# V as the second kind, second sums in four quarters, one power for two, and a reordered loop in a fused graph-transformer kernel

## The reference, cut to what matters

```python
h = logmap0(proj(xn))                       # per row
z = h @ w_qkv                               # 768 channels: q, k, v
t = relu(batchnorm(z))                      # statistics over all 6250 rows
s = grouped_pointwise(depthwise(t))         # groups of 32 channels
ai = rescale(concat(t, s))                  # one factor per row, from the row's sum of squares
q, k = relu(q), relu(k)
vk = einsum('ngdl,ngel->ngde', v, k)        # one position: v * (sum of k over its 32)
out = einsum('ngde,ngdl->ngdl', vk, q) / (sum(v, -1) + 1e-15)
fx = expmap(out_rescaled @ w_res + b_res)
x1 = x + graph + fx
x2 = x1 + experts(layernorm(x1))
```

## Time and profile before

| | us |
|---|---|
| median of 3 runs | 843.91 |
| lowest and highest | 840.88, 845.69 |
| the profiled execution | 845.02 |
| its span | 843.2 |
| TensorE busy | 789.9 |
| VectorE busy | 523.4 |
| ScalarE busy | 424.6 |
| GpSimd busy | 389.2 |

### The profile page before, as it was taken

How to read it: one execution, slowest core, us unless ns; L and a number is a source line. 1 busy time by engine, 2 the same in 40 slices (tenths; PEclk the granted TensorE clock), 3 DMA queues, 4 the chain that set the end, 5 groups by cost and what they waited for, 6 DMA issues and landing times. The chain is left out here.

```text
span 843.2 us, 15014 instructions
## 1 busy us (share of the span) xinstructions
PE 789.9 (94%) x5042; PEld 648.9 (77%) x5042; DVE 523.4 (62%) x1475; ACT 424.6 (50%) x959; POOL 389.2 (46%) x601
## 2 busy tenths in 40 slices
PE   5899999999799999999659889999999999999996
PEld 4678888888466667766436778888888888888885
DVE  7762488797578888788888643534444353535345
ACT  2466436889578888888647232323232323222230
POOL 2430778778068888887636601312222221312122
PEclk9899999999899999999969999999999999999999
DMA  9755122222011110211101040000000000000000
GB/s 213 192 152 152 40 58 56 55 52 52 8 48 43 55 57 25 64 42 51 45 7 33 19 125 13 17 21 22 16 25 13 24 13 25 13 25 14 25 20 30
DMA packets 35422, 41.32 MB, mean 49 GB/s; under 512 B 11520, under 2 KB 20696, under 8 KB 35339
## 3 DMA queue, kind: packets, MB, share of 16 engines
q1 hardware_dynamic: 22355, 30.71, 12.8%
q0 software_dynamic: 8000, 6.82, 3.8%
q10 hardware_dynamic: 4984, 2.79, 1.4%
HBM read 25.59 MB, written 14.60 MB: 48 GB/s over the span
## 5 line engine op out<-in xcount | busy, mean ns | idle before, releaser
L916 ACT ACTIVATE Z<-ps,b1s 128x250 f32<-128x250 f32 x200 | 93.5, 469 | 234.9 <-PE ps L1182 232.1
L1195 PE MATMUL ps<-Z 128*125 128x256 f32 x800 | 176.5, 379 | 0.0
L1182 PE MATMUL ps<-Z 128*128 128x250 f32 x800 | 173.6, 374 | 2.3 <-DMA Z<-in_w 2.3
L1195 PEld LDWEIGHTS ps<-Z 128*125 128x125 f32 x800 | 150.2, 188 | 22.2
L1182 PEld LDWEIGHTS ps<-Z 128*128 128x128 f32 x800 | 151.3, 189 | 20.5 <-DMA Z<-in_w 2.9
L978 PE MATMUL ps<-Z,L 128*128 128x250 f32 x600 | 126.9, 373 | 0.0
L651 POOL TENSOR_SCALAR zr<-zmv 125x1 f32<-125x1 f32 x50 | 11.1, 221 | 250.1 <-issue 240.3
L978 PEld LDWEIGHTS ps<-Z,L 128*128 128x128 f32 x600 | 113.6, 189 | 13.2
L1770 DVE TENSOR_TENSOR Z<-ps,L 125x256 f32<-125x256 f32 x50 | 21.2, 425 | 161.1 <-PE ps L1195 161.1
L1097 PE MATMUL ps<-wr,Z 128*125 128x256 f32 x400 | 92.6, 384 | 0.0
L774 ACT ACTIVATE Z<-Z,bn_o,bn_s 128x250 f32<-128x250 f32 x150 | 80.8, 600 | 1.5 <-DVE bn_o L1481 1.5
(11 more groups left out here) (214 smaller groups left out, 1287.7 us busy)
## 6 DMA issues: line engine op xcount, KB each, us to landing
Z<-in_x SPq DMA_DIRECT2D x25, 250.0 KB
out<-Z SPq DMA_DIRECT2D x24, 250.0 KB
xt_table<-L SPq DMA_DIRECT2D x25, 231.0 KB
Z<-in_x SPq DMA_DIRECT2D x1, 2016.0 KB
g_table<-gt SPq DMA_DIRECT2D x25, 62.5 KB
gr<-g_table SPq DMA_DIRECT2D x25, 62.5 KB
Z<-in_x SPq DMA_DIRECT2D x1, 1344.0 KB
Z<-in_w SPq DMA_DIRECT2D x2, 512.0 KB, 3.4
```

The costliest lines, as they stand in the source:

```text
L916: a_.activation(ge[:, b % 2, f, :], ps[:, f % 4, 0:BT], ACT.Gelu, bias=b1s[:, f // NF, f % NF:f % NF + 1]).then_inc(gelu_done.sem, 1)
L1182: last = mm(ps[:, f % 4, 0:BT], w1s[:, f // NF, k, (f % NF) * 128:(f % NF + 1) * 128], h_of(b, k), start=(k == 0), stop=(k == KD - 1))
L1195: last = mm(ps[0:TP, 4 + 2 * (b % 2) + t, 0:D], ge[:, b % 2, f, t * TP:(t + 1) * TP], w2s[:, f // NF, f % NF, :], start=(f == 0), stop=(f ...
```

## The change

It makes V the second kind and Q the third, so that V's relu runs for 20 blocks inside the rounds and Q's in the loop. `check_t` of 12 blocks moves into the third round, eight more go two by two into the first four steps, the last five stay. The second sums of K go to two banks and use all four quarters; the V products share banks 3 and 4 with the first sums. `turn_xn` stands between `k_sums_s` and `norms`. GpSimd raises the flag first, takes the power for the variance of x1 and that for the squares of u in one instruction, and gathers before it adds the graph part. VectorE reads the flag first in its step. The last `norms` stands ahead of half of the last `res`. Epsilon is spread by a wider transpose and six copies. The second load of the first expert waits until the second expert's first weights have landed. `h` stands at offset 0 of its block, and some small buffers move. The permuting copies double from 12 to 24, and ScalarE's copies of K's weights from 4 to 8.

```diff
-    HOFF = 4 * BT
+    HOFF = 0
...
-        KINDS = (R_K, R_Q, R_V)
-        EARLY_RELU, EARLY_Q = 30, 20
+        KINDS = (R_K, R_V, R_Q)
+        EARLY_RELU, EARLY_V = 30, 20
+        EARLY_CHECK = 12
...
@@ load_expert
+            if i == 0:
+                eng.wait_ge(w1_in[1], 16)
             eng.dma_start(w2s[:, i, :, :], w2[e].rearrange("(k p) f -> p k f", p=128)).then_inc(w2_in[i], 16)
...
@@ gpsimd
+            def powers(k, rows_=True, u_=True):
+                a = k % 2
+                if rows_:
+                    wait_apart(pool, x1, x1.count(k - 1))
+                    g.tensor_scalar(pin[0:TP, a, 0], mv2[0:TP, k - 1, :, 1], LN_EPS, None, ALU.add).then_inc(var_made.sem, 1)
+                if u_:
+                    wait_apart(pool, u_sq, u_sq.count(k))
+                    g.tensor_scalar(pin[0:TP, a, 1], us[0:TP, a], MIN_NORM ** 2, None, ALU.max).then_inc(sq_made.sem, 1)
...
+                g.tensor_tensor(rsu[0:TP, k].rearrange("p r t -> p (r t)")[:, js], pin[0:TP, a].rearrange("p r t -> p (r t)")[:, js],
+                                nhalf[0:TP, js], ALU.pow).then_inc(powered.sem, 1)
...
             steps(NB, [
+                (1, raise_flag),
                 (3, last_scale_of_u),
-                (1, raise_flag),
                 (1, scale_of_norms),
+                (2, gather_piece),
                 (2, lambda b: add_edge(b) if b >= 2 else None),
-                (3, rstd_of_x1),
+                (2, lambda b: powers(b, rows_=b > 0)),
                 (2, scale_of_u),
-                (2, gather_piece),
                 (2, lambda b: add_edge(b) if b < 2 else None),
             ])
...
@@ scalar
             act.wait_ge(bn_done.sem, bn_done.count(2))
-            relu(0, R_V, relu_v)
+            relu(0, R_Q, relu_q)
+            square_s(0, R_V)
             square_t(0)
...
-                (0, ahead(lambda b: relu(b, R_Q, relu_q) if b >= EARLY_Q else None)),
-                (0, ahead(lambda b: relu(b, R_V, relu_v))),
+                (0, ahead(lambda b: relu(b, R_Q, relu_q))),
+                (0, ahead(lambda b: relu(b, R_V, relu_v) if b >= EARLY_V else None)),
                 (1, square_o),
-                (0, lambda b: square_s(b, R_V)),
+                (0, lambda b: square_s(b, R_V) if b else None),
...
             tanh(NB - 3)
+            square_o(NB - 1)
             keep_xn(NB - 4)
-            square_o(NB - 1)
+            keep_norms(NB)
             square_u(NB - 2)
-            keep_norms(NB)
...
@@ tensor
                 for h in range(NH):
                     cv, ck = 2 * R_V + h, 2 * R_K + h
                     for a in range(2):
-                        last_v = quarter(bank_half(R_V, h), pw[:, cv, :], zc(b, cv), a, a)
-                        last_k = quarter(bank_half(3, h), bo, zc(b, ck), a, 1 - a)
+                        last_v = quarter(bank_half(4 - h, 1), pw[:, cv, :], zc(b, cv), a, a ^ h)
+                        last_k = quarter(bank_half(3 + h, 0), bo, zc(b, ck), a, 1 - (a ^ h))
...
@@ k_sums_s
-                for h in range(NH):
-                    for a in range(2):
-                        last = quarter(bank_half(4, h), bo, skr[:, h * BT:(h + 1) * BT], a, a)
-                last.then_inc(kss_done.sem, 1)
+                for a in range(2):
+                    last_0 = quarter(bank_half(1, 0), bo, skr[:, 0:BT], a, a)
+                    last_1 = quarter(bank_half(2, 0), bo, skr[:, BT:2 * BT], a, 1 - a)
+                last_0.then_inc(kss_done.sem, 1)
+                last_1.then_inc(kss_done.sem, 1)
...
             steps(NB, [
+                (0, lambda b: None if b else pointwise_v(b)),
                 (0, pointwise_kq),
                 (1, turn_norms),
                 (2, res),
+                (0, lambda b: pointwise_v(b) if b else None),
+                (0, k_sums_s),
                 (4, turn_xn),
-                (0, pointwise_v),
-                (0, k_sums_s),
                 (0, norms),
             ])
...
             turn_xn(NB - 4)
+            norms(NB)
             res_half(NB - 1, 0)
-            norms(NB)
             turn_norms(NB)
...
@@ vector
+            def more_checks(s):
+                for b in range(EARLY_CHECK + 2 * s, min(EARLY_CHECK + 2 * s + 2, EARLY_V)):
+                    check_t(b)
...
             for n in range(3 * NB):
...
+                if EARLY_RELU + NB < n <= EARLY_RELU + NB + EARLY_CHECK:
+                    check_t(n - 1 - EARLY_RELU - NB)
...
@@ divide_where_needed
-                    for q in range(4):
-                        w = min(32, TP - 32 * q)
-                        for p in range(4):
-                            alone(v_.tensor_copy(eb.rearrange("p (t n) -> p t n", t=TB)[32 * p:32 * p + 32, :, 32 * q:32 * q + w],
-                                                 ebt[32 * q:32 * q + 32, 1, :, 0:w]), q == 3 and p == 3)
+                    alone(v_.transpose(eb, den[:, 0:TB * 128]))
+                    places = eb.rearrange("p (t q c) -> p t q c", t=TB, q=4)
+                    alone(v_.tensor_copy(places[64:128, :, 0:2], places[0:64, :, 0:2]), False)
+                    alone(v_.tensor_copy(places[0:64, :, 2:4], places[64:128, :, 2:4]))
                     for q in range(4):
+                        p = q ^ 1
+                        alone(v_.tensor_copy(places[32 * q:32 * q + 32, :, p % 2:4:2], places[32 * p:32 * p + 32, :, p % 2:4:2]),
+                              q == 3)
...
+                    alone(v_.tensor_copy(eb[0:HALF, 0:BT], vk[HALF:128, 0:BT]), False)
+                    alone(v_.tensor_copy(eb[HALF:128, 0:BT], vk[0:HALF, 0:BT]))
...
             def make_xn(b):
-                dve.wait_ge(rstd_done.sem, rstd_done.count(b))
+                dve.wait_ge(rows_pow.sem, rows_pow.count(b))
...
             steps(NB, [
+                (0, lambda b: check_t(b) if b >= EARLY_V else None),
+                (1, divide_where_needed),
                 (3, make_x1),
-                (0, check_t),
-                (1, divide_where_needed),
                 (3, sums_of_x1),
                 (0, keep_k),
                 (3, moments_of_x1),
                 (2, make_u),
+                (0, attend_s),
                 (0, check_s),
                 (0, attend_t),
-                (0, attend_s),
+                (0, more_checks),
                 (3, make_xn),
                 (0, keep_turned),
                 (0, late_now),
             ])
```

More of the change, by code:

```diff
@@ L213, in gps_layer @@
         spill = take(D // 2).bitcast(BF16)
-        eb = take(BT)
+        eb = take(TB * 128)
         den = take(NH * BT)
@@ L227, in gps_layer @@
         yo = take(2 * TB * D).rearrange("p (a t d) -> p a t d", a=2, t=TB)
+        rt = take(19 * (EX + 1))[0:1].rearrange("p (i e) -> p i e", i=19)
         take = cut((0, LW, L))
@@ L1025, in pointwise_v @@
                     idle_work(7, 4)
+                pe.wait_ge(relu_k.sem, relu_k.count(b))
+                pe.wait_ge(relu_q.sem, relu_q.count(b))
+                if b:
+                    pe.wait_ge(s_sq.sem, s_sq.count(b - 1))
+                    pe.wait_ge(q_kept.sem, q_kept.count(b - 1))
+                    pe.wait_ge(k_kept.sem, k_kept.count(b - 1))
+                    pe.wait_ge(att.sem, att.count(b - 1, 1))
+                else:
+                    pe.wait_ge(z_kept.sem, 3 * NB - 7 + R_K)
+                for h in range(NH):
+                    cq, ck = 2 * R_Q + h, 2 * R_K + h
+                    for a in range(2):
+                        quarter(bank_half(R_Q, h), pw[:, cq, :], zc(b, cq), a, a)
+                        last = quarter(bank_half(R_K, h), pw[:, ck, :], zc(b, ck), a, 1 - a)
+                last.then_inc(s_done.sem, 1)
+            def pointwise_v(b):
                 if b == 1:
-                    idle_work(7, 2)
+                    idle_work(7, 3)
                     pe.wait_ge(nrm_kept.sem, nrm_kept.count(0))
@@ new lines, in divide_where_needed @@
+                    halves = ((tokens(zc(b, 2 * R_V, 2)), den), (ps[:, 3:5, BT:2 * BT].rearrange("p h (t n) -> p h t n", t=TB), vk))
+                    for n, (v, d) in enumerate(halves):
+                        alone(v_.tensor_tensor(tokens(d), v, eps, ALU.add), n == 1)
+                    for n, (_, d) in enumerate(halves):
+                        alone(v_.reciprocal(d, d), n == 1)
+                    for n, (v, d) in enumerate(halves):
+                        alone(v_.tensor_tensor(tokens(d), v, tokens(d), ALU.mult), n == 1)
```

232 lines of the change are left out of this document (120 added, 112 removed).

## The result

| | before | changed |
|---|---|---|
| median of 20 runs, us | 842.73 (840.88 to 846.73) | 846.14 (842.74 to 850.46) |
| profiled execution, us | 845.02 | 845.47 |
| its span, us | 843.2 | 843.5 |

The ratio is 1.0032 with a 95% interval of 1.0017 to 1.0048: about 2.7 us slower, inside the 0.5% that I had called "the same". The forecast was 831.3 us, with 821 to 841 as its range. It was wrong by some 14 us, and so was the sign.

What follows compares the result with a forecast made beforehand. TensorE was taken to bound the loop, the other engines close behind. Common steps -8.1, disturbed step -2.2, start -0.7, end -0.7 and experts -2.0 sum to -13.7 us: from 845.02 to 831.3 us, range 821 to 841.

Steps and rivals of the forecast that it cites:

- The ring: In each loop step, GpSimd and VectorE wait for each other through merged power, make_xn, check and flag: 8.52 to 9.03 us.
- the disturbed step: The one block that sets the flag and is divided: -2.2 us, between -3.5 and 0.
- TensorE's step: TensorE's own common loop step: from 9.20 to 8.80 us, by -0.50 for second sums and +0.10 for a change of shape.
- C: Rival: the quarters of the second sums do not run side by side; 837.9 us; chance 0.13 shared with the port rival.
- the irregular part: Time of the mean loop step above its bound: 0.17 us before, put at 0.10 after, as cheaper work gives cover.
- The copies: In the disturbed block: six copies for sixteen, wider transpose and copy, swap of halves, one more product: net -1.1 us.
- The start: Start of the loop: late statistics +2.5, order of first products -1.5, clock -1.7; sum -0.7 us, between -3.2 and +3.5.
- The end: End of the loop: last norms earlier by about 1 us, partly taken back by the graph part; -0.7, between -2 and +0.5.
- The experts: TensorE's 2.00 us wait for the second expert's first weights goes: -2.0 us, between -2.7 and 0.
- B: Rival: contention at the VectorE-GpSimd port lengthens power and graph part, step 9.2; 837.9 us; chance 0.13 shared with the quarters rival.
- D: Rival: within 0.5%, port contention or serial quarters plus a start of +3.5 and an end of 0; about 842.8 us; chance 0.09.
- E: Rival: slower, power, powers of the norms and graph part all meet VectorE's two-operand work, ring 9.9; 853.3 us; chance 0.06.

Runs made afterwards that it cites:

- both removals: Changed kernel with the power for x1's variance taken by itself again and the gathering DMA behind the scale of u: ratio 0.9952 to the kernel before.
- powers apart and old order: Changed kernel with x1's variance power by itself, last scale of u ahead of the flag, make_x1 ahead of the flag's read: ratio 0.9975 to the kernel before.
- powers apart, DMA last and the old end: Changed kernel with x1's variance power by itself, gathering DMA behind the scale of u, GpSimd's old order at the loop's end: ratio 0.9938 to the kernel before.
- the run with the old end: GpSimd's old order at the loop's end, added to separate powers and the old order around the flag: ratio 0.993 to the kernel before.

## Why the prediction was wrong, point by point

**The ring (the step that failed).** Of the 14 us, 10.5 lie in the common steps of the loop (-8.1 forecast, +2.4 measured), 4.6 in the disturbed step and 2.2 at the end; a start better by 1.3 and the 2.0 of scatter stand against them. In the common steps the ring was named, its pieces were right, and its bound was set wrongly: "between 8.80 and 9.03 I take 8.90". In the step shown above the pieces are: last scale and gathering DMA 0.84 + 1.39 = 2.23 (put at 1.96); flag and powers of the norms up to the graph part 0.45 + 2.05 = 2.50 (2.13); graph part 1.52 (1.51); the two small operations 0.67 (0.60); the merged power to `make_xn` 1.47 (1.08 + 0.05); `make_xn` to the check 0.84 (0.89); check to flag 0.43 (0.30). Together 9.66 against 8.52. The largest misses are the power with its port contention (0.34, inside the 0.51 allowed for it) and the gaps between GpSimd's instructions, which I had read off a step in which they were short or which I had not put in: 0.50 us from L608's start to the gathering DMA's, 0.56 us for the last scale's first operation (0.24 in the next step). None is large; a ring adds them all. I had allowed contention at one place and these gaps at none. The prediction's own mark, "wrong if the ring is over 9.4 us", was met in a part of the steps; at 9.1 to 9.4 in most others the gain was gone already. With both removals the intervals without the disturbed one fall from 218.9 to 214.1 us, so the ring costs 4.8 of the 10.5 us.

**TensorE's step.** Second sums 0.53 us instead of 0.95, with their change of shape, for which 0.55 was put: right, and C is refuted. The step is 8.92, not 8.80: the turned rows take 0.58 instead of 0.53, turned norms and `res` 4.09 instead of 3.99, the rest 0.03 less than forecast. The 2.00 us from V to norms are no wait for the square of V: it ends 1.82 us after V, and in the steps before the first turned rows, where only it stands in the way, norms start at 1.91. (My 1.88 for V to norms had left out the change of shape that I counted elsewhere.)

**What lies above TensorE's step (a second term mis-sized).** I counted cheaper work as cover and put the irregular part at 0.10 us a step. By the measure of that forecast, turned norms of block 1 to 20, the kernel with powers apart and the DMA last has a mean of 9.29 us, 0.37 above TensorE's 8.92; before the change it was 0.17 above 9.20. So even with the ring out of the way the common steps give back 2.4 us (216.5 to 214.1) and not 8.1. All of it comes in the fifteen intervals of the middle (139.7 to 137.3 us). The first five (49.1 and 49.2) and the last three (27.7 and 27.6) give nothing: something other than TensorE sets them. Six checks moved from the first steps into the round shorten the first five intervals by 0.9 us; what the rest of them waits for stays open.

In some steps ScalarE's square of V starts only 1.35 to 1.8 us after V though ScalarE is idle and waits for TensorE by the trace (1.77 in the kernel with powers apart and old order, at 326.80 us). What releases it so late stays open, and no run tested it.

**The disturbed step.** Forecast -2.2, measured +2.4; TensorE stands still for 16.5 us where 14.4 was foreseen. Two steps failed. The copies: the swap of halves, L1642, takes 1.77 us in the changed kernel and 0.25 us where the gathering DMA stands elsewhere.

```profile
414.92 1.35 POOL L580 DMA_INDIRECT xg<-xt_table,idst  x1 [0.30 <-issue]
415.35 1.77 DVE L1642 COPY L<-L 64x128 f32<-64x128 f32 x1
```

```profile
412.66 0.25 DVE L1641 COPY L<-L 64x128 f32<-64x128 f32 x1
```

(The second is from the kernel with powers apart, DMA last and the old end.) The copy starts 0.43 us behind the DMA's issue on GpSimd and ends long after it. It takes 1.56 to 1.77 us in all eight kernels of this study with the new copies in which it meets that issue, and 0.25 or 0.26 in the seven in which it doesn't. The Trainium skill ("SBUF — State Buffer", Who interferes with whom) says that a copy in a two-port mode blocks fully while GpSimd holds the shared pair; these rows agree, though the copy ends 0.85 us after the DMA's issue does, and what holds it so long is not shown: GpSimd's graph part starts at 416.31, but beside the graph part alone the same copy takes the 0.25 us above. From widening the value to the first sum of the division the changed kernel takes 4.31 us, the other 2.77, the kernel before 4.60; foreseen were 4.60 - 2.25 + 0.4, some 2.8. So the copies were priced rightly as long as no gathering DMA meets them. The other step is the start of the division: it was to come 1.1 us earlier, and comes 0.90 us later (2.36 us after the flag instead of 1.46), because the powers of the norms stand behind the flag and the last scale on GpSimd. Up to the squares of the divided block this makes +1.30 us (18.48 against 17.18). The +1.07 behind it is within the scatter of the clock's return, which had no term. The windows of the changed kernel (PE busy, granted clock) and of the kernel without the wait for weights, whose loop is the same code:

```profile
434.00:436.00 2.00, 2.00 (x19) 0.50 0.00 0
436.00:438.00 2.00, 2.00 (x32) 0.75 0.00 0
```

```profile
434.00:436.00 2.00, 2.00 (x36) 1.15 (x34) 1.94 (x5) 1.25 (x7) 1.03 (x2) 1.00 0.00 0
436.00:438.00 2.00, 2.00 (x30) 1.28 (x23) 1.47 (x4) 1.66 (x3) 0.57 (x2) 1.00 0.00 0
```

TensorE stands still for 14.5 to 16.5 us during the division, its granted clock falls to 0.50, from 2.4 to 1.2 GHz, and it is back at 1.00 some 3.3 us after V in the second of these executions and 6.9 us after V in the first. From the flag up to the second sums both are the same to 0.02 us; the next flag comes 28.19 and 26.51 us after the last. A scatter of 1.7 us with the same code is more than the +1.07, which therefore says nothing of the change.

**The start.** Forecast -0.7, measured -2.0. Late statistics: from the rounds' end to the variance 3.75 us instead of 2.03, so +1.7 for the 2.5 foreseen; with 2 checks in the round it is 2.02 again. The clock: right in full.

```profile
216.37 1.89 PE L1122 MATMUL ps<-L,ones 128*32 128x250 f32 x24
```

The first norms take 1.89 us at a granted clock of 1.00, against 3.56 in the earlier trace rows; that is -1.67. The rest, some -2.1 where I had put -1.5 for the order of the first products, is a remainder that no run tested.

**The end.** Forecast -0.7, measured +1.5. I had seen the graph part before the last scale and priced it at a part of 1 us; I had not seen that the powers of the last norms, for which GpSimd waits, were moved ahead of the power for u. The run with the old end gave back 1.2 us there and 0.6 behind it.

**The experts.** Forecast -2.0, measured -1.7, of which the wait itself is 0.9 to 1.5.

**The rivals.** B, the port, was the nearest in mechanism, and its 837.9 us was no longer slow enough; D (842.8) had the time for other reasons. E had the sign and the ring that runs away, but not its way: it asked for meetings with VectorE's products at three places, and of these the powers of the norms took 1.02 us in every step from 240 to 400 us and the graph part 1.4 in all but one; only the power met them. The mean of 9.53 us lies under the 9.77 that it asked for, and the end and the disturbed step did the rest. A ring slower than 9.03 should have carried more of the range: with half of E's price the ring is 9.2, the mean 9.3 and the time 838.3; with the end at +0.5 and the disturbed step at 0, both bounds of my own, 841.7. That alone passes the upper end of 841, and the measured ring of up to 9.66 lies between this and E's 9.9.

## What to carry to other kernels

A change that merges two steps of a chain to save an instruction ties their inputs together; ask which wait the earlier one now inherits, and follow from there until you are back at the start. If you get back, it is a ring, and its length is the sum of everything in it, gaps and contention too: take it from start to start of neighbouring instructions in the slowest step that you can find, not from durations in a good one, and compare it with the step of the bound before you count any gain there. Compare a mean over the stretch on which the forecast was made: here the middle steps alone hide the loss at the ends of the loop. And test a gain on the bound by putting its cost back: where that costs nothing, something else sets the pace.

## What the runs showed of the hardware that I had not expected

- Contention between VectorE and GpSimd is moved by another order more easily than removed: 0.3 us went from the power (median 1.05 instead of 1.36 us) to the small operation ahead of it (median 0.55 instead of 0.23).
- A copy of 64 x 128 from SBUF to SBUF on VectorE takes 0.25 us away from GpSimd's issue of a gathering DMA and 1.56 to 1.77 us when it starts during it, in eight kernels.
- After the same idle time of 16.5 us, TensorE's granted clock was back at 1.00 some 3.3 us after V in one execution and 6.9 us after V in another, though the two had been alike to 0.02 us from the flag to the second sums.
